# Shared down-projection scales from sums of squares on GpSimd, and a reordered passage from attention to the token tiles

## The reference

```python
x = x + attention(layernorm(x), ctx, ctx)   # 32 query heads, 8 key/value heads of 16, then @ Wfc.T + bfc
h = layernorm(x)                            # 2048 x 512
scores = softmax(h @ gate_weight.T)         # 8 experts, the best 2 of 2 groups
routed = sum over the 2 chosen experts of  w * (silu(h @ gate_w.T) * (h @ up_w.T)) @ down_w.T   # F = 352
shared = (silu(h @ sh_gate.T) * (h @ sh_up.T)) @ sh_down.T                                      # 2 x 352
out = x + routed + shared
```

## Time and profile before

| | us |
|---|---|
| median of 3 runs | 774.12 |
| lowest and highest | 771.83, 774.58 |
| profiled execution, its own time | 773.04 |
| its span, first to last instruction | 771.3 |

### The profile page before, as it was taken

How to read it: one execution, slowest core, us unless ns; L and a number is a source line. 1 busy time by engine, 2 the same in 40 slices (tenths; PEclk the granted TensorE clock), 3 DMA queues, 4 the chain that set the end, 5 groups by cost and what they waited for, 6 DMA issues and landing times.

```text
span 771.3 us, 15970 instructions
## 1 busy us (share of the span) xinstructions
PE 748.0 (97%) x5151; PEld 404.5 (52%) x5152; DVE 567.5 (74%) x1194; ACT 424.4 (55%) x860; POOL 267.4 (35%) x222
## 2 busy tenths in 40 slices
PE   6998999999999999999999999999999999999997
PEld 4553533444444335666655656555555555555554
DVE  5777779999999977887689886555555555446767
ACT  3666568988888875776624543343434343323231
POOL 3263007999995303657000101111111111016331
PEclk9999989999999999999999999999999999999999
DMA  9898846575655799996678556777777779549995
GB/s 331 336 406 252 252 158 202 170 208 170 181 178 158 248 356 331 367 381 224 192 203 243 138 134 160 178 180 177 180 177 177 180 180 216 128 110 280 306 259 164
DMA packets 161336, 171.04 MB, mean 222 GB/s; under 512 B 103616, under 2 KB 117440, under 8 KB 160768
## 3 DMA queue, kind: packets, MB, share of 16 engines
q1 hardware_dynamic: 149724, 128.36, 57.0%
q0 software_dynamic: 10960, 40.90, 17.1%
q10 hardware_dynamic: 596, 1.07, 0.4%
HBM read 104.87 MB, written 42.21 MB: 191 GB/s over the span
## 4 chain that ended last, share of the span: by engine, by line
PE 77%; DVE 13%; DMA 5%; issue 2%; ACT 2%; SPq 1%; ACTq 0%; DVEq 0%
PE psum L1500 31%; PE psum L1512 17%; DVE sb_rows L1732 6%; PE psum L1430 5%; PE psum L1349 5%; PE psum L1239 4%; PE psum L1335 4%; PE psum L1263 3%; DMA sb_weights<-in_wdn 2%; PE psum L1215 2%; DMA sb_weights<-in_x 1%; PE psum L1366 1%; PE psum L1448 1%; PE psum L1220 1%; DMA x_dram<-sb_rows 1%
## 5 line engine op out<-in xcount | busy, mean ns | idle before, releaser
L1500 PE MATMUL psum<-sb_weights,sb_rows 128*128 (+1 forms) x1608 | 250.8, 313 | 0.0
L1500 PEld LDWEIGHTS psum<-sb_weights,sb_rows 128*128 128x128 f16 x1608 | 157.3, 98 | 91.1 <-DMA sb_rows<-xnT_dram 0.3
L1732 DVE TENSOR_REDUCE sb_rows<-psum 128x4 f32<-128x1024 f32 x128 | 149.9, 1215 | 5.4 <-PE psum L1263 5.4
L1054 ACT ACTIVATE sb_weights<-psum 128x512 f32<-128x512 f32 x256 | 139.2, 595 | 23.5 <-PE psum L1335 20.5
L1512 PE MATMUL psum<-sb_weights,sb_hT 128*128 (+1 forms) x630 | 147.2, 379 | 0.0
L918 POOL DMA_INDIRECT sb_rows<-xn_rows,sb_slot_tok x39 | 38.4, 985 | 217.7 <-DVE sb_rows L2325 147.8
L1512 PEld LDWEIGHTS psum<-sb_weights,sb_hT 128*128 128x128 f16 x630 | 61.6, 98 | 64.8
L1128 ACT ACTIVATE psum<-psum 128x352 f32<-128x352 f32 x71 | 31.8, 448 | 114.4 <-DVE psum L1986 104.0
L1335 PE MATMUL psum<-sb_weights 50*128 50x512 f16 x256 | 87.0, 390 | 2.3 <-ACT sb_weights L1054 1.4
L1349 PE MATMUL psum<-sb_weights 128*32 128x256 f32 x1024 | 83.1, 397 | 0.3
L1263 PE MATMUL psum<-sb_weights 48*128 48x256 f16 x512 | 71.8, 275 | 0.7 <-DVE sb_rows L1732 0.7
(11 more groups left out here) (275 smaller groups left out, 1016.8 us busy)
## 6 DMA issues: line engine op xcount, KB each, us to landing
sb_weights<-in_wgu SPq DMA_DIRECT2D x20, 704.0 KB, 7.9
sb_weights<-in_wgu POOLq DMA_DIRECT2D x20, 704.0 KB, 6.0
sb_weights<-in_wdn SPq DMA_DIRECT2D x17, 768.0 KB, 6.4
slot_y<-sb_rows SPq DMA_DIRECT2D x39, 256.0 KB, 2.3
sb_weights<-q_parts SPq DMA_DIRECT2D x96, 64.0 KB, 2.8
x_dram<-sb_rows SPq DMA_DIRECT2D x24, 256.0 KB, 4.2
q_parts<-sb_weights SPq DMA_DIRECT2D x16, 256.0 KB, 4.0
sb_rows<-in_x POOLq DMA_DIRECT2D x16, 256.0 KB, 5.4
```

Of the source, the lines that this page charges most:

```text
L1054: nc.scalar.activation(probs[G % 2][:, kt, pair * 512:(pair + 1) * 512], bank[4 + f % 2], ACT.Exp, scale=exp_by[n]).then_inc(exp_done, 1)
L1500: mm = nc.tensor.matmul(bank[GU_BANKS[par][which]][:, 0:F], x_T[:, xp * D + k * P:xp * D + (k + 1) * P], gu(wp, k, which), start=(k == 0 a ...
L1732: nc.vector.tensor_reduce(to[:, :, j // UB, :, j % UB, qt], psum[:, banks[qt] * 512:(banks[qt] + 2) * 512] .rearrange("p (a h k) -> p a h ...
```

## The change

- The shared down matrices are loaded first, into places of their own (`load_shared_down`), and GpSimd sums their squares (`shared_sum`: one multiplication, eight halvings and a last addition for each matrix). It does so ahead of the bias additions 13 and 15. VectorE takes a maximum over three partial sums and roots it approximately (`shared_tops`) in place of maxima 8 and 9. `dn_max_done` is complete at 9.
- The ring has three places and eight loads: 0 after `nm_rows(14)`, 1 and 2 after `nm_rows(15)`, 3 to 7 after `store_attn(13)` and the attention loads.
- The first two `ot_transpose` come at the ends of groups 61 and 62, and their copies ahead of the last `attn_out`; the third comes after the last `pair_transpose`, ahead of the second projection.
- `normalise(62)` moves into `residual_norm(0)`, and `store_attn(15)` behind the first `store_x2`.
- The maxima are transposed behind the second projection and back behind the third; `down_scales` follows `residual_norm(2)`; ScalarE's wait for it moves from t = 2 to t = 4. TensorE's wait for `scale_done` at t = 3 (L1472) is as it was.

```diff
@@ -122,12 +122,13 @@
             return words(DN0 + slot * DN_W, DN_W)
-        RING = (0, 1, 2, 3, 4, 0, 1, 3, 2, 0)
-        RING_AFTER = {5: 0, 6: 1, 7: 3, 8: 2, 9: 5}
+        RING = (0, 1, 2, 0, 1, 2, 0, 1)
+        RING_AT = (DN0 + DN_W, 8 * MG * HH * BT // 2, 8 * MG * HH * BT // 2 + DN_W)
+        RING_TURN = len(RING_AT)
         def ring(i):
-            return dn_raw(RING[i]) if RING[i] < 3 else words(8 * MG * HH * BT // 2 + (RING[i] - 3) * DN_W, DN_W)
+            return words(RING_AT[RING[i]], DN_W)
         def ring_turn(i):
             return RING[:i].count(RING[i])
...
@@ -289,6 +289,9 @@
         h_sb = [sb(f"h{i}", [P, FP]) for i in range(2)]
         h16 = [h[:].bitcast(F16).rearrange("p (s f) -> p s f", s=2) for h in h_sb]
         silu_out = [h[:].rearrange("p (s f) -> p s f", s=2)[:, :, 0:F // 2] for h in h_sb]
+        w_max_rows = h_sb[0][0:NE + SH, 0:P]
+        dn_sums = half_max[:, 2:2 + SH * NF].rearrange("p (c j) -> p c j", c=SH)
         def two_parts(bank_):
             return bank_[:, 0:F].rearrange("p (s f) -> p s f", s=2)
...
@@ -467,11 +471,15 @@
             def load_ring(i):
-                if i in (3, 4):
+                if RING_AT[RING[i]] in RING_AT[1:]:
                     sp.wait_ge(pv_ready, 3 * UNITS * UG // BLOCKS)
-                if i in RING_AFTER:
-                    sp.wait_ge(dn_max_done, RING_AFTER[i] + 1)
+                if i >= RING_TURN:
+                    sp.wait_ge(dn_max_done, i - RING_TURN + 1)
                 sp.dma_start(ring(i), wdn[i]).then_inc(ring_ld[RING[i]], 16)
+            def load_shared_down(c):
+                sp.dma_start(dn_raw((NE + c) % 3), wdn[NE + c]).then_inc(sh_ld, 16)
             def load_down(e):
@@ -553,7 +561,10 @@
             for u in range(12, 16):
                 if u + 2 < UNITS:
                     nm_rows(u + 2)
-                for i in {12: (0, 1, 2), 13: (3, 4)}.get(u, ()):
+                if u == 12:
+                    for c in range(SH):
+                        load_shared_down(c)
+                for i in {12: (0,), 13: (1, 2)}.get(u, ()):
                     load_ring(i)
                 if u == 15:
@@ -565,7 +576,8 @@
                     load_attn(0, 3)
                     sp.wait_ge(ota_ready, 1)
                     load_attn(1, 0)
-                store_attn(u)
+                if u < UNITS - 1:
+                    store_attn(u)
                 if u == 13:
                     for s in range(2):
@@ -574,10 +586,8 @@
                     for r in range(3):
                         load_attn(0, r)
                 if u == 13:
-                    for i in (5, 6, 7, 8):
+                    for i in range(RING_TURN, NE):
                         load_ring(i)
-                if u == 14:
-                    load_ring(9)
@@ -600,10 +610,12 @@
                 sp.wait_ge(ota_ready, t + 2)
                 load_attn(1, t + 1)
                 store_x2(t, t)
-                store_xn2(t, t)
                 if t == 0:
+                    store_attn(UNITS - 1)
+                else:
                     sp.wait_ge(attn_st[1], FREE + 16 * BATCH)
                     load_res_rows(1, 1)
+                store_xn2(t, t)
             def token_tile(t):
                 s = t % 2
@@ -852,6 +864,22 @@
                 load_cut(c)
             bias_order = list(range(2, TILES)) + [0, 1]
+            squares, SUM_STEPS, SUMS_SEEN = words(P1_0, DN_W), 10, (BLOCKS - 2) * TPB
+            def shared_sum(c):
+                raw, done = dn_raw((NE + c) % 3), SUMS_SEEN + SUM_STEPS * c
+                nc.gpsimd.tensor_tensor(squares, raw, raw, ALU.mult).then_inc(fc_square, 1)
+                n, done = DN_W // 2, done + 1
+                pool.wait_ge(fc_square, done)
+                while n > NF:
+                    nc.gpsimd.tensor_tensor(squares[:, 0:n], squares[:, 0:n], squares[:, n:2 * n], ALU.add).then_inc(fc_square, 1)
+                    n, done = n // 2, done + 1
+                    pool.wait_ge(fc_square, done)
+                nc.gpsimd.tensor_tensor(dn_sums[:, c, :], squares[:, 0:NF], squares[:, NF:2 * NF],
+                                        ALU.add).then_inc(fc_square, 1)
+                pool.wait_ge(fc_square, done + 1)
             def load_x(i):
                 if i >= 2:
                     pool.wait_ge(xb_st[i % 2], i // 2 * 16)
@@ -871,6 +899,10 @@
                 if t < CUTS_P2:
                     pool.wait_ge(nm_done, t + 3)
                     cut_weights(t)
+                if t in (TILES - 3, TILES - 1):
+                    c = (t - TILES + 3) // 2
+                    pool.wait_ge(sh_ld, 16 * SH)
+                    shared_sum(c)
                 if t + 1 < TILES:
                     load_x(t + 1)
                 add_bias(t)
@@ -890,7 +922,7 @@
                 part.then_inc(dn_cut, 1)
             pool.wait_ge(attn_done, UNITS * UG)
-            pool.wait_ge(dn_max_done, NE + SH)
+            pool.wait_ge(dn_max_done, NE + 1)
             for h in range(3):
                 load_held(h)
             for c in range(CUTS_P2, CUTS):
@@ -1081,10 +1113,11 @@
             act.wait_ge(gu_cut, CUTS_P2)
             ot_evac(0, 0)
+            ot_evac(1, 1)
             attn_out(UNITS * UG - 1)
             nc.scalar.activation(warm, ident[:, 0:TPB], ACT.Sqrt)
+            ot_evac(2, 0)
             for t in range(2):
-                ot_evac(t + 1, (t + 1) % 2)
                 std2(t)
                 ln2_out(t, t)
             def dn_first(e, pieces):
@@ -1109,7 +1142,7 @@
                     gate_out(t - 3, (t - 3) % 2)
                 if t - 2 < 2 * HELD:
                     first_part(t - 2)
-                if t == 2:
+                if t == 4:
                     act.wait_ge(scale_done, 2)
                 if 2 * HELD + 2 <= t < 2 * HELD + 2 + SH:
                     e = NE + t - 2 * HELD - 2
@@ -1366,6 +1399,17 @@
                         tr = nc.tensor.transpose(bank[7][:, (2 * b + qt) * P:(2 * b + qt + 1) * P],
                                                  o_raw[(G + b) % 4][:, qt * P:(qt + 1) * P], ident[:])
                 tr.then_inc(ot_ready, 1)
+            def ot_transpose(t, r, n):
+                s = r % 2
+                pe.wait_ge(a_ld[r], n * 16 + (16 + A_SEEN))
+                if isinstance(t, int) and t == 0:
+                    pe.wait_ge(max_done, UNITS * 2 * UG)
+                if not (isinstance(t, int) and t < 2):
+                    pe.wait_ge(ota_evac, t - 1)
+                for k in range(KD):
+                    tr = nc.tensor.transpose(bank[s][:, k * P:(k + 1) * P], a_in[r][:, k * P:(k + 1) * P], ident[:])
+                tr.then_inc(ota_ready, 1)
             pe.wait_ge(rest_done, KQ * BLOCKS + 1)
             unit_ready(2, 2, 0)
@@ -1411,16 +1455,10 @@
                     pe.wait_ge(w_max_b, 1)
                     nc.tensor.transpose(bank[7][:, P:P + NE + SH], w_max_first,
                                         ident[0:NE + SH, 0:NE + SH]).then_inc(w_max_tt, 1)
+                if G >= UNITS * UG - 3 and G < UNITS * UG - 1:
+                    i = G - UNITS * UG + 3
+                    ot_transpose(i, i, 0)
             LAST = UNITS * UG - 1
-            def ot_transpose(t, r, n):
-                s = r % 2
-                pe.wait_ge(a_ld[r], n * 16 + (16 + A_SEEN))
-                if not (isinstance(t, int) and t < 2):
-                    pe.wait_ge(ota_evac, t - 1)
-                for k in range(KD):
-                    tr = nc.tensor.transpose(bank[s][:, k * P:(k + 1) * P], a_in[r][:, k * P:(k + 1) * P], ident[:])
-                tr.then_inc(ota_ready, 1)
             def out_project(t, s):
                 pe.wait_ge(ota_evac, t + 1)
@@ -1449,23 +1487,14 @@
                                           start=(k == 0), stop=(k == KD - 1))
                 mm.then_inc(gate_ready, 1)
-            pe.wait_ge(max_done, UNITS * 2 * UG)
-            ot_transpose(0, 0, 0)
             pv_part(LAST, 1)
-            ot_transpose(1, 1, 0)
             pe.wait_ge(w_fc, 48)
-            for t in range(2):
-                if t == 1:
-                    ot_transpose(2, 2, 0)
-                out_project(t, t)
-                if t == 0:
-                    pair_transpose(LAST - 1)
-                    pe.wait_ge(dn_max_done, NE + SH)
-                    nc.tensor.transpose(bank[5][0:NE + SH, 0:P], dn_max[:], ident[:]).then_inc(w_max_t, 1)
-                else:
-                    pe.wait_ge(w_max_b, 2)
-                    nc.tensor.transpose(bank[5][:, P:P + NE + SH], w_max_rows,
-                                        ident[0:NE + SH, 0:NE + SH]).then_inc(w_max_tt, 1)
+            out_project(0, 0)
+            pair_transpose(LAST - 1)
+            ot_transpose(2, 2, 0)
+            out_project(1, 1)
+            pe.wait_ge(dn_max_done, NE + 1)
+            nc.tensor.transpose(bank[5][0:NE + SH, 0:P], dn_max[:], ident[:]).then_inc(w_max_t, 1)
             for t in range(2, 4):
                 if t == 3:
```

(29 more changed lines are left out.)

## The result

| | before | after |
|---|---|---|
| median of 4 runs, us | 772.98 | 791.6 |
| lowest and highest, us | 770.93, 774.58 | 790.02, 794.76 |
| profiled execution, us | 773.04 | 790.02 |
| its span, us | 771.3 | 788.3 |
| mean granted clock of TensorE | 0.995 | 0.985 |

The ratio is 1.0251, with a 95% interval from 1.022 to 1.0282: 18.6 us slower. The forecast was slower by 11.9, at 786 with a range up to 791; the sign was right and the size too small. What has to be found is the term that is 7 us short.

The account below looks back on a forecast made before the run. TensorE, busy for 97% of the span, was taken as the bound, so only its waits count. Terms 9.2 - 1.5 + 4.1 = 11.8 us on the median of 774.12 gave 785.9, taken as 786, with a range from 779 to 791.

Parts of the forecast that it names:

- the ring's +9.2: Last attention groups: weight loads land one reader later, normalisations come late, and the transposes at 276.17 are delayed 9.2 us.
- the passage's -1.5: First to third projection: 9.2 us instead of 10.46, with two maxima and one normalisation removed ahead; 1.5 us gained.
- the +4.1 of the wait that moves: Ahead of `ln_transpose(1)`: TensorE stands 4.2 us for scales now formed behind the third projection; 4.1 us slower.
- pair(56): TensorE's transposes at 270.68 in the last attention groups, forecast to wait 4.0 us for VectorE's normalisation ending at 274.7.
- pair(58): TensorE's transposes at 276.17 in the last attention groups, forecast to wait for a normalisation until 285.4, 9.2 us late.
- Step 1: Third early weight load, read by VectorE's maximum 0: taken to land at 264.3 (bounds 262.5 and 265.5), against 262.44 before.
- Steps 2 and 4: Ring load 1 lands 4.7 us after issue, at 272.3; ring load 3 lands 6.0 after issue, at 283.0.
- GpSimd, 0 while covered: GpSimd's sums of the shared parts: 10.2 us each, second ending near 291, covered by 7 us before the first residual.
- The ring's own upper bound, +15.8: Last attention groups: delay of the transposes at 276.17 with the latest first landing (265.5) and slowest loads (7.3, 8.8).

Follow-up runs that it names:

- before, ring late: Kernel before, with load 0 alone behind nm_rows(14), loads 1 and 2 behind nm_rows(15), 3 to 8 behind the attention loads; 782.37 us, ratio 1.0114.
- before, late scales: Kernel before, with the down scales formed behind residual_norm(2) instead of residual_norm(1) and ScalarE's wait at t = 4; 781.58 us, ratio 1.0104.
- after, scales mended: Changed kernel, with the maxima's transposes in bank 7, TensorE's scales wait behind tile 4's projection, and GpSimd's held cuts behind scale_done 2; 782.62 us.
- after, ring first: Changed kernel, with ring loads 0 to 2 ahead of the shared parts behind nm_rows(14), and 3 and 4 behind nm_rows(15); 790.31 us, ratio 1.0224.
- after, all mended: Changed kernel, with bank 7, held cuts behind scale_done 2, ring loads 0 and 1 ahead of the shared parts, sums ahead of bias additions 14 and 15; 772.53 us.

## Why the size was wrong: the forecast's steps

Passages (one trace each) and medians together:

| kernel | passage, us | median, us |
|---|---|---|
| before | 39.63 | 773.1 |
| after | 58.25 | 791.6 |
| before, ring late | 48.36 | 782.37 |
| before, late scales | 51.40 | 781.58 |
| after, scales mended | 48.10 | 782.62 |
| after, ring first | 59.18 | 790.31 |
| after, all mended | 37.96 | 772.53 |

By the passages, ring +8.7, scales +11.8 and all mended -1.7 make 18.8 of the 18.6; by the medians, 9.2, 8.4 and -0.6 make 17.0. The close fit of the first sum is partly luck: the scales' mending takes 10.2 us off the passage after, and the 11.8 hold a projection of 5.60 us at the low clock where the kernel after has 4.33. The second sum is 1.6 short, within the intervals of its terms (1.4 to 2.7 us to either side).

The forecast's own terms against the trace after, up to tile 4: +9.3 for the ring's +9.2, -1.3 for the passage's -1.5, and +10.7 for the +4.1 of the wait that moves. The whole miss is in the last.

- **The ring, +9.2: right in place, and in size partly by luck.** pair(56) waited 2.53 us where 4.0 was forecast, pair(58) is 7.9 late and not 9.2, and 1.3 more come up to the first projection, for which TensorE ran at a mean clock of 0.54 between 272 and 286 (eight value products took 1.08 us instead of 0.64). Step 1 took maximum 0 to be nearly 2 us late; the third load landed in 7.8 us, not 10.2, and it waited 0.68. Steps 2 and 4 took 4.7 and 6.0 us to landing; it was 4.5 and 6.5. The clock, which the forecast left out without a reason, filled the difference.
- **GpSimd, 0 while covered: right.** A sum took 8.4 us (2.74, 5.28, 0.19 and gaps), 10.2 forecast, since its smallest instructions cost 0.19 to 0.3 and not 0.37. The second ended at 282.94, 13 us ahead of the first residual, and not near 291. The ring-first experiment shows what it costs when that cover is taken away: nearly all that the ring gives.
- **The passage, -1.5: right as far as tile 4.** The first to the third projection took 9.15 us, 9.2 forecast, against 10.46. The forecast took it for a lasting gain; with everything mended it was gone by tile 8.
- **The wait that moves, +4.1: this term failed.** That TensorE stands for the scales was right; two things in its size were not. In the trace it is 9.2 up to `ln_transpose(1)` and 1.4 behind it, 10.7 in all. The sum took the scales' four instructions at the 0.66 us that they had at 297, where GpSimd was idle. At their new place GpSimd is cutting, and they took 5.6. The forecast looked at who waits for the scales and not at who works beside them. The other 1.4 us are the clock behind the wait, which the sum put at nothing; filling the wait gave 1.3 of them back.
- The range ended at 791, 0.6 us short. The ring's own upper bound, +15.8, would have put it at 792.5 (774.1 + 15.8 - 1.5 + 4.1), but for the wrong reason. No bound was given to VectorE's instructions at the new place. Rows for them existed, but from a place where GpSimd was idle, and such rows are no bound.

The page of the Trainium skill that bears on this is SBUF — State Buffer, Who interferes with whom: a `tensor_scalar` from SBUF to SBUF can enter a mode that uses both port pairs of VectorE, one of which GpSimd shares, and whichever is issued first has it for the whole instruction while the other stands. The trace agrees: VectorE's instructions end at 311.39 and 314.33, each within 0.03 us of the end of GpSimd's, 311.37 and 314.30. The scale instruction that reads PSUM took 0.16 us, but it began at 308.74, 0.1 us ahead of GpSimd's first cut, and so tests nothing here.

## What to carry to other kernels

A short instruction has the price of its row only while its neighbours stay the same: when you move one, look at what every other engine does at the new moment, and for VectorE at GpSimd first. When a reader is added in front of a queue of loads, price every later reader one place later, and ask what in-order work stands behind each. And when mending one wait leaves the time as it was, look for the work that the wait had covered before dropping the theory.

## What the runs showed of the hardware

- VectorE's `TENSOR_SCALAR` on 128 x 10 int32 from SBUF to SBUF took 0.17 us with GpSimd idle and 2.46 and 2.82 us when issued just behind the start of a GpSimd `TENSOR_TENSOR` of 2.53 and 2.86 us. One on 128 x 2 took 1.14 us instead of 0.17, beside a GpSimd addition of 1.26 (the ring-first kernel). One on 128 x 1 was not held: in the kernel before it takes 0.15 us at 306.06, inside a GpSimd instruction that runs from 305.05 to 307.91. Nor was a `TENSOR_TENSOR` with one input in PSUM and one in SBUF: 0.69 us at 303.23 in the kernel before, inside a GpSimd instruction from 302.44 to 304.97.
- After waits of 2.8 to 9.1 us in the token tiles TensorE's work ran slower for several us: 1.11 or 1.12 us for four transposes instead of 0.66, and 4.30 to 5.60 us for the projection behind them instead of 3.6. The length of the wait didn't set the loss: the projection took 4.30 behind 2.78 us, 5.29 behind 3.99, 4.33 behind 8.93 and 5.60 behind 9.10. Filling the wait of 8.93 with unread transposes kept the clock at 1.00.
- GpSimd's two-input instruction on three elements takes 0.19 us, so the line through 512 and 1536 elements, with 0.37 at its foot, is too high for small ones.
